# One-hots of the routing tile by tile, the inversion between sums of turns, and gathers between masks

## The reference, cut to what matters

```python
x = L0_attn_u
xn = _layernorm(x, axis=-1)
x = x + attn(xn, W_in, W_out, dt_bias, B_bias, ...) + ffn(xn, Wr, br, W1, W3, W2, gamma, beta)

# ffn
probs = softmax(xf @ Wr + br);  vals, idx = top_k(probs, 2);  w = vals / vals.sum()
for ei in range(16):
    h = silu(xf @ W1[ei]) * (xf @ W3[ei]);  y = layernorm(h @ W2[ei]) * gamma[ei] + beta[ei]
    out = out + combine[:, ei:ei + 1] * y

# attn: theta = cumsum(angles * dt); K, Q = rope(rmsnorm(B) + B_bias, theta), rope(rmsnorm(C) + C_bias, theta)
#       decay = exp(ell_i - ell_j) for i >= j;  S = (Q K^T) * decay;  y = S x + Q H;  out = (y + D x) * silu(z) @ W_out
```

## Time and profile before

| | |
|---|---|
| runs, median | 284.9 us |
| the profiled execution | 283.92 us, span 282.2 us |
| granted TensorE clock, mean | 0.973 of full |
| TensorE matmul busy | 252.1 us, 89% of the span |
| VectorE busy | 221.4 us, 78% |
| GpSimd busy | 208.3 us, 74% |
| ScalarE busy | 150.0 us, 53% |
| chain that ended last | TensorE 60%, VectorE 17%, ScalarE 6%, issue 6%, DMA 4%, GpSimd 4% |

### The profile page before, as it was taken

One profiled execution on the slowest core, in us unless ns is written; L12 is line 12 of the kernel. 1 busy time (PEld: TensorE's weight loads), 2 busy tenths in 40 slices (PEclk: granted clock), 3 DMA queues, 4 the chain that ended last, 5 costly groups with the idle time before them and its releaser, 6 DMA issues.

```text
span 282.2 us, 7396 instructions
## 1 busy us (share of the span) xinstructions
PE 252.1 (89%) x2157; PEld 217.9 (77%) x2161; DVE 221.4 (78%) x604; ACT 150.0 (53%) x512; POOL 208.3 (74%) x284
## 2 busy tenths in 40 slices
PE   2999997799999999999999999999999999999600
PEld 0857964787897998899889979997998899889500
DVE  4778998778787969796979688787969796978446
ACT  1766996593456453755364645456453745363033
POOL 8656997698887787888887878887787875665400
PEclk9999999799999999999999999999999999999965
DMA  5630888665779778977889687988878987870096
GB/s 155 224 94 7 273 261 286 173 187 164 208 228 281 253 224 250 275 234 221 250 288 237 232 249 202 303 245 270 262 225 242 274 245 231 255 220 30 21 264 182
DMA packets 68856, 61.55 MB, mean 218 GB/s; under 512 B 6609, under 2 KB 52305, under 8 KB 68817
## 3 DMA queue, kind: packets, MB, share of 16 engines
q1 hardware_dynamic: 66256, 55.83, 65.5%
q0 software_dynamic: 2560, 5.25, 6.5%
HBM read 56.27 MB, written 4.78 MB: 216 GB/s over the span
## 4 chain that ended last, share of the span: by engine, by line
PE 60%; DVE 17%; ACT 6%; issue 6%; DMA 4%; POOL 4%; SPq 1%; DVEq 1%; POOLq 0%; ACTq 0%
PE bank L874 16%; PE bank L917 6%; PE bank L817 5%; PE bank L809 4%; PE bank L869 4%; PE bank L801 3%; PE bank L763 2%; PE bank L851 2%; PE bank L768 2%; DMA decay<-res_dram 2%; PE bank L913 2%; DVE rot L1360 2%; DVE sd L1376 2%; PE bank L833 2%; PE bank L860 1%
## 5 line engine op out<-in xcount | busy, mean ns | idle before, releaser
L874 PE MATMUL bank<-blkT,w_up 128*128 128x128 f32 x512 | 64.7, 280 | 1.5 <-DVE xrow L1410 0.6
L874 PEld LDWEIGHTS bank<-blkT,w_up 128*128 128x128 f32 x512 | 61.4, 195 | 4.2 <-issue 2.3
L633 POOL DMA_INDIRECT res_dram<-xrow,sidx x40 | 40.7, 1017 | 21.9 <-DVE xrow L1438 17.7
L580 POOL DMA_INDIRECT blk<-xn_dram,gidx x40 | 42.7, 1067 | 8.5 <-issue 7.3
L917 PE MATMUL bank<-w,xrow 128*128 128x128 f32 x256 | 34.6, 278 | 0.3 <-DVE xrow L1425 0.3
L1113 ACT ACTIVATE xrow<-bank 128x512 f32<-128x512 f32 x40 | 25.2, 629 | 15.2 <-PE bank L874 11.2
L917 PEld LDWEIGHTS bank<-w,xrow 128*128 128x128 f32 x256 | 31.1, 192 | 1.6 <-issue 1.6
L1410 DVE TENSOR_TENSOR xrow<-xrow,bank 128x512 f32<-128x512 f32 x40 | 27.3, 682 | 4.4 <-issue 4.2
L1342 DVE SCALAR_TENSOR_TENSOR kq<-sd,rms,bias_kq 128x512 f32<-128x512 f32 x32 | 23.2, 765 | 8.5 <-POOL rms L591 7.5
L626 POOL TENSOR_TENSOR rstd<-mv,mhalf 128x1 f32<-128x1 f32 x40 | 25.2, 629 | 0.3
L1107 ACT ACTIVATE blkT<-bank 128x128 f32<-128x128 f32 x40 | 12.2, 306 | 24.5 <-PE bank L860 20.9
(11 more groups left out here) (250 smaller groups left out, 617.1 us busy)
## 6 DMA issues: line engine op xcount, KB each, us to landing
w_up<-in_L_ffn_W_dram SPq DMA_DIRECT2D x96, 256.0 KB
w<-in_L_ffn_W_dram SPq DMA_DIRECT2D x48, 256.0 KB
e_row<-e_dram SPq DMA_DIRECT2D x16, 256.0 KB
decay<-l_dram SPq DMA_DIRECT2D x4, 512.0 KB, 6.0
gam<-in_L_ffn_gamma_dram SPq DMA_DIRECT2D x32, 64.0 KB
shift_y<-in_L_ffn_beta_dram SPq DMA_DIRECT2D x32, 64.0 KB
acc<-in_L_attn_u_dram SPq DMA_DIRECT2D x4, 256.0 KB, 3.7
xn_dram<-xrow SPq DMA_DIRECT2D x4, 256.0 KB, 5.1
```

Of the source, the lines that this page charges most:

```text
L580: g.indirect_dma_start(out=blk[:, b % SLOTS, :], out_offset=None, in_=xn_dram, in_offset=bass.IndirectOffsetOnAxis(ap=gidx[:, entry(b):ent ...
L633: g.indirect_dma_start(out=res_dram, in_=res[:, b % HALF, :], in_offset=None, out_offset=bass.IndirectOffsetOnAxis(ap=sidx[:, entry(b):ent ...
L874: last = m(bank[out][:, c * P:(c + 1) * P], w_up[:, u % SETS, n, c * P:(c + 1) * P], blkT[:, b % 2, :], start=True, stop=True)
```

## The change

It does four things.

- The one-hots are made tile by tile: for each of the 32 groups one instruction compares the row of block numbers with the token's block and multiplies by the token number, both scalars of each partition, and one compares the row of lanes with the token's lane. The fp16 copies of the scalars go, and so does a cast on GpSimd. The semaphore `hot_ready` counts every 8 tiles, and `invert` waits for each 8. The cast of the experts (`blk_e`) comes ahead of the one-hots. The two selections of slots become one instruction and one reduction over both choices.
- `invert(1)` comes ahead of `sum_turns(2)`; `mean_square(0)` and `cut_turns(0)` come ahead of VectorE's wait for the inversion, `cut_turns(3)` behind `rotate(0)`; the three warm-up matmuls ahead of block 0 go.
- GpSimd's `gather(0)` comes ahead of the mask of the last decay row; ScalarE's logarithm for the decays comes ahead of the counts of experts.
- In tile 1: ScalarE takes `squares` first, and `out_block` and `silu` of the first block ahead of its weighing; VectorE takes `norm_kq` behind `product(b0)`; GpSimd takes the product `weigh_q(0)` behind `rms_pow(1)`.

```diff
-        lg, rt, sc1, posb, pick = (scratch([P, NT, NE]) for _ in range(5))
+        rt, posb = (scratch([P, NT, NE]) for _ in range(2))
+        pick = scratch([P, TOPK, NT, NE])
+        lg, sc1 = pick[:, 0], pick[:, 1]
...
-        oh1 = scratch([P, NT, NE])
-        oh2 = scratch([P, NT, NE])
+        chosen = scratch([P, TOPK, NT, NE])
+        oh1, oh2 = chosen[:, 0], chosen[:, 1]
... GpSimd
-            link(g.iota(val[:, NT:], [[-P, NT]], ...))
-            g.tensor_copy(val_h, val)
+            g.iota(val[:, NT:], [[-P, NT]], ...)
...
-            for t in range(SUMMED, NT):
+            for t in range(SUMMED, NT - 1):
                 cut_rows(t)
             pool.wait_ge(xn_out, 16 * NBATCH)
             pool.wait_ge(gidx_ready, 1)
+            gather(0)
+            cut_rows(NT - 1)
...
-            gather(0)
             gather(1)
             rms_pow(0)
...
                     rms_pow(t)
+                if t == 1:
+                    weigh_q(0)
...
-                if first:
+                if first and t > 0:
                     weigh_q(t)
... TensorE
             def invert(k):
-                pe.wait_ge(hot_ready, k + 1)
                 for t in range(NT):
                     q = k * NT + t
+                    if t % 8 == 0:
+                        pe.wait_ge(hot_ready, q // 8 + 1)
...
             invert(0)
             sum_turns(1)
+            invert(1)
             sum_turns(2)
-            invert(1)
             sum_turns(3)
...
                 pe.wait_ge(sidx_ready, 1)
-                for _ in range(WARM_BLOCKS):
-                    m(bank[6][:, :], ones_h[:, :], neg_h[:, :, :].rearrange("p h i -> p (h i)"), start=True, stop=True)
                 turn_block(0)
... ScalarE
+            act.wait_ge(g_ready, 1)
+            a(lnG, gmax, ACT.Ln).then_inc(lng_ready, 1)
             act.wait_ge(ends_ready, 1)
...
-            act.wait_ge(g_ready, 1)
-            a(lnG, gmax, ACT.Ln).then_inc(lng_ready, 1)
...
-                if first:
+                if t == 1:
+                    squares(t)
+                    sines(t)
+                    out_block(b0 + 1)
+                    silu(b0)
+                elif first:
                     sines(t)
                     squares(t)
+                if first:
                     weigh(t)
... VectorE
-            tt(pick, oh1, posb, ALU.mult)
-            link(tt(sc1, oh2, posb, ALU.mult))
-            v.tensor_reduce(slot[:, 0, :], pick, X, ALU.add)
-            link(v.tensor_reduce(slot[:, 1, :], sc1, X, ALU.add))
+            link(tt(pick, chosen, bc(posb, TOPK, 0), ALU.mult))
+            link(v.tensor_reduce(slot, pick, X, ALU.add))
...
-            v.tensor_copy(blk_h, s_blk)
-            link(stt(lan_h, s_blk, -float(P), slot, ALU.mult, ALU.add))
-            def one_hots(k):
-                q0, q1 = k * NT, (k + 1) * NT
-                link(tt(row_h[:, q0:q1, :], bc(iota_k, NT, 0), bc(blk_h[:, k, :], NB, 1), ALU.is_equal))
-                if k == 0:
-                    dve.wait_ge(expert_psum, 1)
-                    v.tensor_copy(blk_e[:, :], bank[3][0:1, 0:NU]).then_inc(blk_e_ready, 1)
-                tt(row_h[:, q0:q1, :], row_h[:, q0:q1, :], bc(val_h[:, q0:q1], NB, 1), ALU.mult)
-                tt(lane_h[k], bc(iota_l, NT, 0), bc(lan_h[:, k, :], P, 1), ALU.is_equal).then_inc(hot_ready, 1)
-            one_hots(0)
-            one_hots(1)
+            link(stt(s_lane, s_blk, -float(P), slot, ALU.mult, ALU.add))
+            dve.wait_ge(expert_psum, 1)
+            v.tensor_copy(blk_e[:, :], bank[3][0:1, 0:NU]).then_inc(blk_e_ready, 1)
+            for k in range(TOPK):
+                for t in range(NT):
+                    q = k * NT + t
+                    ts(row_h[:, q, :], iota_k, s_blk[:, k, t:t + 1], val[:, q:q + 1], ALU.is_equal, ALU.mult)
+                    last = ts(lane_h[k][:, t, :], iota_l, s_lane[:, k, t:t + 1], None, ALU.is_equal)
+                    if t % 8 == 7:
+                        last.then_inc(hot_ready, 1)
+            mean_square(0)
+            cut_turns(0)
             dve.wait_ge(perm_psum, 1)
... begin of VectorE
-                mean_square(0)
-                for b in range(NBATCH - 1):
-                    cut_turns(b)
+                cut_turns(1)
+                cut_turns(2)
...
                 product(0)
-                cut_turns(NBATCH - 1)
                 rot_cosine(0)
                 rotate(0)
+                cut_turns(3)
                 product(1)
... iteration of VectorE
-                    norm_kq(t)
+                    if t > 1:
+                        norm_kq(t)
                 if b0 is not None:
...
                     product(b0)
+                if t == 1:
+                    norm_kq(t)
```

More of the change, by code:

```diff
@@ L55, in build @@
     WARM_ROUTING = 3
-    WARM_BLOCKS = 3
     ARMS = (4, 5, 7)
@@ L198, in build @@
         dump = scratch([P, NB])
-        val_h = scratch([P, NQ], fp16)
-        blk_h = scratch([P, TOPK, NT], fp16)
-        lan_h = scratch([P, TOPK, NT], fp16)
         lrow = scratch([P, P])
@@ L505, in _ @@
             g.iota(val[:, 0:NT], [[P, NT]], base=1, channel_multiplier=1, allow_small_or_imprecise_dtypes=True)
-            link(g.iota(val[:, NT:], [[-P, NT]], base=-1, channel_multiplier=-1, allow_small_or_imprecise_dtypes=True))
-            g.tensor_copy(val_h, val)
+            g.iota(val[:, NT:], [[-P, NT]], base=-1, channel_multiplier=-1, allow_small_or_imprecise_dtypes=True)
             g.iota(dump[:, :], [[P, NB]], base=DUMP, channel_multiplier=1, allow_small_or_imprecise_dtypes=True)\
@@ L1148, in iteration @@
                     if b is not None:
-                        out_block(b + 1)
-                        silu(b)
+                        if t > 1 or b is not b0:
+                            out_block(b + 1)
+                            silu(b)
                         out_h(b - 1)
@@ L1240, in _, with cut_turns, mean_square @@
             link(tt(wtop[:, 1, :], wtop[:, 0, :], e2, ALU.mult))
+            def cut_turns(b):
+                sums = bank[THETA[b]]
+                dve.wait_ge(theta_psum, b + 1)
+                cut = turns[:, b * TB:(b + 1) * TB, :].rearrange("p j c -> p (j c)") if b >= 2 else cut_[b]
+                link(ts(cut, sums[:, :], MAGIC, -MAGIC, ALU.add, ALU.add))
+                tt(theta[:, b * TB:(b + 1) * TB, :].rearrange("p j c -> p (j c)"), sums[:, :], cut,
+                   ALU.subtract).then_inc(theta_ready, 1)
+            def mean_square(t):
+                dve.wait_ge(s["sq_done"], 2 * (t + 1))
+                again(dve, s["rms_ready"], t)
+                ts(ms[:, :], ms[:, :], 1.0 / DS, EPS, ALU.mult, ALU.add).then_inc(s["ms_ready"], 1)
             def pick_experts():
@@ L1311, in _ @@
             tt(sidx[:, :], v_row, v_neg, ALU.add).then_inc(sidx_ready, 1)
-            def cut_turns(b):
-                sums = bank[THETA[b]]
-                dve.wait_ge(theta_psum, b + 1)
-                cut = turns[:, b * TB:(b + 1) * TB, :].rearrange("p j c -> p (j c)") if b >= 2 else cut_[b]
-                link(ts(cut, sums[:, :], MAGIC, -MAGIC, ALU.add, ALU.add))
-                tt(theta[:, b * TB:(b + 1) * TB, :].rearrange("p j c -> p (j c)"), sums[:, :], cut,
-                   ALU.subtract).then_inc(theta_ready, 1)
             def diagonal(t):
@@ L1327, in diagonal @@
                     .then_inc(decay_done, 1)
-            def mean_square(t):
-                dve.wait_ge(s["sq_done"], 2 * (t + 1))
-                again(dve, s["rms_ready"], t)
-                ts(ms[:, :], ms[:, :], 1.0 / DS, EPS, ALU.mult, ALU.add).then_inc(s["ms_ready"], 1)
             def norm_kq(t):
```

## The result

The change makes the kernel slower: 288.0 us (287.62 to 288.51, 4 runs) against 284.61 (284.07 to 285.16), a ratio of 1.012, 95% interval 1.009 to 1.015. The forecast was 287.0 with a range of 282.5 to 291.0. All ratios compare fast runs alone: one execution of a later version took 429.01 us at a mean granted TensorE clock of 0.56 and is left out, as is one of 287.1 of the kernel before.

A forecast was written before the change was run, and what follows sets the result against it. TensorE's blocks bound from 75 us to the end; before, VectorE's routing and the first gather. -0.7 + 2.6 + 2.3 + 0.75 - 0.9 + 0.5 - 1.2 - 0.6 = +2.75 gave 287.0; 8-in-10 range 282.5 to 291.0 us.

The forecast's parts named there:

- Step 1: Selection and rounding on VectorE before the first one-hot: 3.2 us instead of 3.87, so 0.7 saved.
- Step 2: One-hots on VectorE: 32 pairs at 0.39, 12.5 us for 9.9, plus 2.3 of waits on GpSimd.
- rival of cheap scalars: One-hots with scalar instructions 0.14 apart end no later than now: about -2.0, 282 to 283 us; chance 0.20.
- Step 3: Before the token list: mean_square(0) and cut_turns(0) ahead of VectorE's wait delay list, gather and all blocks, +0.75.
- Step 4: First gather: takes 2.9 us instead of 3.82, as the weights start earlier, -0.9.
- Step 5: TensorE before and in the first blocks: half clock on the sums +0.5, first blocks at full clock -1.2.
- Step 6: Reordered tile 1 on VectorE, ScalarE and GpSimd: aims at TensorE's 0.65 stall, -0.6.
- term of cut_turns(3): Cut behind rotate(0) on VectorE: delays product(1) by about 1.0, needed by TensorE a stage later, so 0.

The follow-up runs named there:

- second trace of the changed kernel: The changed kernel with 28 extra VectorE instructions near its end, where VectorE and GpSimd are idle: 287.52 us in one run.
- three things undone: The changed kernel with wide one-hots, cut_turns(0) behind the lists and cut_turns(3) ahead of rot_cosine(0): 284.14 us, ratio to before 0.997.

## Why the prediction was right, step by step

The forecast of +2.75 for the profiled execution came out as +3.7, 1 us more. The terms:

| step | forecast | measured |
|---|---|---|
| 1 up to the first one-hot | -0.7 | +0.2 |
| 2 one-hots, instructions | 12.5 | 11.6 |
| 2 one-hots, waits for GpSimd | 2.3 | 1.8 |
| 3 ahead of the list | +0.75 | +0.6 |
| 4 gather | -0.9 | -1.0 |
| 5 sums and clock | +0.5 and -1.2 | 0 and -1.3 |
| 6 keys of tile 0 | | +0.8 |
| 6 on to the queries of tile 1 | -0.6 in all | +0.3 |
| 6 tile 2 and after | | +0.8 |

- Step 1 failed by 0.9. The selection itself saved 0.6 as worked out; but GpSimd's turns, brought on by the earlier logarithm, which I counted only as fewer masks beside the one-hots, now stand beside the position arithmetic ahead of it, and L1288 and L1293 take 0.9 longer there. The logarithm was not moved alone.
- Step 2, which decided the sign, was right in kind and 1.4 too dear: the pair is 0.36, not 0.39, and the masks cost 1.8 in all, five of them 0.36 each, not 0.45. The bounds held it, and the rival of cheap scalars falls with the prices: its point of decision was a pair of 0.31. The cycle table of the Trainium skill ("VectorE: DVE Perf Modes", the TRN2 errata), from which I had made a pair 0.17 as an estimate, holds nothing for the scalars, and the 0.18 measured with immediates is near it. The exclusive lock of the Trainium skill ("SBUF — State Buffer", the shared port pair) agrees with 13.4 against 11.6 us.
- Step 3: 1.30 from the last one-hot to the read, for 0.68, where 0.75 more was forecast. Undoing it moved the list by 0.78 and TensorE's last instruction by 0.56 in the trace, yet not the time beyond its spread.
- Step 4 was right: 2.79 for the forecast 2.9. That the emptier DMA engines are the reason was not tested alone, but six traces fit it: the gathers of before, of the wide one-hots and of the run with matmuls of ones take 3.82, 4.26 and 4.30 us with the DMA engines 84 to 95% busy, those of the changed kernel, the small one-hots alone and sum_turns(2) ahead 2.79, 2.79 and 2.82 with 8 to 23%.
- Step 5 came near by luck. The first blocks gained 0.86 and 0.42, as forecast, and the sums lost nothing, because in the profiled execution the half clock fell on sum 1, a place that I had not named. In the second trace of the changed kernel it fell on sum 2, as the forecast had it, and block 0 started 0.34 later, at 53.75. And of the 1.28 gained on the blocks a part is no gain: TensorE reaches the keys of tile 0 that much sooner, but the rotation ends only 0.57 sooner after block 0 is turned (7.11 us for 7.68).
- Step 6 failed. The step that failed is the term of cut_turns(3), put at 0 because TensorE needs product(1) a stage later. It also delays the products on VectorE and GpSimd that the keys of tile 1 need, and costs 1.1 to 1.3 us up to the queries of tile 1. The wait of 0.69 at the keys of tile 1 that I had laid to the late norm_kq goes with it. The moved steps of tile 1 gain 1.0 there in the changed kernel, more than the 0.6 forecast, and give back 0.5 in tile 2, which I had not counted. The wait of 0.79 at the keys of tile 0 is not from the moved steps: the run with the small one-hots alone has 0.72 there, and it is the other side of the faster blocks of step 5. The last 0.3, behind the queries of tile 2, lies within the 0.4 by which that stretch differs among the traces.

The sign and the deciding step were right in their mechanism. That the number came so near was luck in part, by misses of both signs: step 2 too dear by 1.4 and step 5 better by 0.6 than forecast, steps 1 and 6 too cheap by 0.9 and 2.5.

## What to carry to other kernels

Before a wide broadcast is split into small instructions, take the pitch of the small form from the trace, with its scalars: here 0.08 to 0.10 us for one without them, 0.06 for each scalar of a partition, and 0.36 on the mean for each mask of GpSimd that lies beside. A faster streaming rate is worth little where 128 elements take some 0.03 us of 0.165 (an estimate from the 0.02 between 40 and 128). When an engine's work is moved earlier, look at what it then stands beside; when it is moved later, follow every engine that waits behind it, not only TensorE.

## What the runs showed of the hardware

- The granted clock of TensorE falls to 0.50 once, for 3 to 4 us between 41 and 56 us, in eleven of the thirteen traces of this study. In one it does not fall (three things undone), and in the one with the masks held back it is low from 44.3 to 51.1 and again from 58.0 to 61.4. Where it falls differs even for the same code: on sum 1 in the changed kernel (hidden), on sum 2 in its second trace (block 0 at 53.75 for 53.41). On block 0 it costs up to 1.6 (3.63 us for 16 matmuls, for 2.02).
- Each fall begins within an idle stretch of TensorE of 1.7 to 2.5 us (4.9 in one), or up to 1.7 us behind one; but some such stretches pass without a fall, as the 2.43 ahead of block 0 with sum_turns(2) ahead. So a single trace of before and one of after cannot be compared by this term. It is likely a part of the spread of 2 to 3 us among the runs of one kernel, which was not shown.
- GpSimd's masks of 128x512 take 0.60 us each with VectorE idle (4.17 for seven, masks held back), 0.64 beside VectorE instructions of 0.2 us, and 1.21 or 2.68 beside broadcasts of 1.0 to 1.25 and of 2.7. Small VectorE instructions hardly delay GpSimd; VectorE pays, 0.36 us for each mask.
